# Layer 0's expert weights loaded in five transfers, four of them paced by the row scatters, and one program block for all parts behind attention 0

## The reference, cut to what matters

```python
for e in range(N_EXPERTS):                       # 16 experts, each token goes to 2
    h = silu(flat @ Wu[e]) * (flat @ Wg[e])
    out = out + combine[:, e:e + 1] * (h @ Wd[e])
for s in range(N_SHARED):
    out = out + silu(flat @ Su[s]) * (flat @ Sg[s]) @ Sd[s]
...
x = x + ffn0(layernorm(x))                       # layer 0, then
x = x + attn1(layernorm(x))                      # layer 1's attention
```

## Time and profile before

| what | value |
|---|---|
| time, median of 3 runs | 1125.06 us (1124.02 to 1129.27) |
| the profiled execution's own time | 1130.29 us |
| its span, from the first to the last instruction | 1128.6 us |
| PE busy | 889.0 us, 79% |
| DVE, POOL, ACT busy | 687.4, 632.6, 467.2 us |
| granted TensorE clock, mean | 0.849 |

### The profile page before, as it was taken

One profiled execution on the slowest core, in us unless ns is written; L12 is line 12 of the kernel. 1 busy time (PEld: TensorE's weight loads), 2 busy tenths in 40 slices (PEclk: granted clock), 3 DMA queues, 4 the chain that ended last, 5 costly groups with the idle time before them and its releaser, 6 DMA issues.

```text
span 1128.6 us, 22056 instructions
## 1 busy us (share of the span) xinstructions
PE 889.0 (79%) x5927; PEld 689.5 (61%) x5927; DVE 687.4 (61%) x2668; ACT 467.2 (41%) x1176; POOL 632.6 (56%) x878
## 2 busy tenths in 40 slices
PE   1578888888597899268888788997599999999900
PEld 0456666665554788156666556564488888888700
DVE  5688898774553355366788666354255555555578
ACT  2336566554310344145665444331144444444400
POOL 3646666533137356375558888877366665665600
PEclk9769899897889899556989877598699999999955
DMA  7600000000253553700001222277555555555287
GB/s 214 225 1 1 1 2 1 1 2 2 80 225 109 149 151 104 261 0 1 2 1 72 83 94 100 100 246 293 200 173 175 179 177 174 175 171 169 69 355 314
DMA packets 72965, 136.97 MB, mean 121 GB/s; under 512 B 13278, under 2 KB 51597, under 8 KB 70800
## 3 DMA queue, kind: packets, MB, share of 16 engines
q1 hardware_dynamic: 52016, 85.15, 23.3%
q0 software_dynamic: 17632, 46.73, 11.6%
q10 hardware_dynamic: 3200, 3.70, 0.9%
HBM read 79.15 MB, written 62.39 MB: 125 GB/s over the span
## 4 chain that ended last, share of the span: by engine, by line
PE 32%; POOL 11%; DVE 8%; issue 5%; DMA 2%; ACT 1%; POOLq 0%; DVEq 0%; SPq 0%; ACTq 0%
PE s_psum L2047 12%; POOL rows L1577 7%; PE s_psum L2060 6%; PE s_psum L2039 3%; DVE f_rows L2148 2%; DVE f_xT L2148 2%; DVE a_masked L1089 2%; PE s_psum L2055 2%; POOL a_probs L1436 1%; PE s_psum L649 1%; DMA rows<-f_rows,f_place_at 1%; PE s_psum L552 1%; PE s_psum L605 1%; PE s_psum L585 1%; PE s_psum L632 1%
## 5 line engine op out<-in xcount | busy, mean ns | idle before, releaser
L2159 POOL DMA_INDIRECT parts<-e_y,e_dest x206 | 202.6, 984 | 154.8 <-issue 121.6
L2047 PE MATMUL s_psum<-wres,e_xT 128*128 x824 | 215.1, 384 | 0.3 <-ACT e_xT L2088 0.2
L1436 POOL TENSOR_SCALAR_AFFINE_SELECT a_probs<-a_probs 128x256 f32<-128x256 f32 x256 | 108.7, 449 | 120.1 <-ACT a_probs L873 119.6
L2047 PEld LDWEIGHTS s_psum<-wres,e_xT 128*128 128x128 f32 x824 | 158.1, 193 | 22.6 <-issue 1.1
L1577 POOL DMA_INDIRECT rows<-f_rows,f_place_at x128 | 125.3, 979 | 36.3 <-issue 32.3
L873 ACT ACTIVATE a_probs<-s_psum 128x768 f32<-128x768 f32 x128 | 104.6, 817 | 75.2 <-PE s_psum L632 73.5
L2093 ACT ACTIVATE e_act_out<-s_psum 128x128 f32<-128x128 f32 x206 | 57.2, 278 | 178.1 <-PE s_psum L2047 178.1
L2122 DVE TENSOR_TENSOR e_hid<-e_act_out,s_psum 128x128 f32<-128x128 f32 x206 | 59.5, 289 | 113.2 <-PE s_psum L2055 84.2
L2060 PE MATMUL s_psum<-wres,e_hT 128*128 x412 | 123.6, 382 | 0.0
L1089 DVE CUSTOM_DVE_ANT_0 a_masked<-s_psum,a_ahead 128x128 f32<-128x128 f32 (+1 forms) x256 | 76.0, 353 | 42.7 <-PE s_psum L608 42.2
L2131 DVE TENSOR_SCALAR e_y<-s_psum,e_xg 128x256 f32<-128x256 f32 x206 | 99.7, 484 | 1.0 <-issue 1.0
(11 more groups left out here) (299 smaller groups left out, 1993.1 us busy)
## 6 DMA issues: line engine op xcount, KB each, us to landing
e_xg<-rows SPq DMA_DIRECT2D x159, 160.0 KB, 2.3
f_rows<-parts SPq DMA_DIRECT2D x8, 1024.0 KB, 7.3
f_xT<-parts SPq DMA_DIRECT2D x8, 1024.0 KB, 7.8
wres<-in_experts SPq DMA_DIRECT2D x21, 384.0 KB, 5.7
e_xg<-rows SPq DMA_DIRECT2D x47, 144.0 KB, 2.2
wres<-in_experts SPq DMA_DIRECT2D x4, 1536.0 KB
rows<-empty SPq DMA_DIRECT2D x1, 5120.0 KB, 24.5
parts<-e_y,e_dest POOLq DMA_INDIRECT x206, 2.4
```

The costliest lines, as they stand in the source:

```text
L1436: last = nc.gpsimd.affine_select(out=diagonal[:, :, a], in_=diagonal[:, :, a], compare_op=ALU.is_ge, fill=0.0, base=0, pattern=[[0, 2], [1 ...
L2047: last = nc.tensor.matmul(ps_u[b % 2][:, 0:2 * P], xT[b % 2][:, c * P:(c + 1) * P], wres[:, ds(e, 1), 2 * c * P:2 * (c + 1) * P].rearrange ...
L2159: nc.gpsimd.indirect_dma_start(out=parts[:, :], out_offset=bass.IndirectOffsetOnAxis(ap=dest[b % NY][:], axis=0), in_=y[b % NY][:], in_off ...
```

## The change

In `dispatch`, SP now loads experts 0 to 7 in one transfer at the stage's start, and experts 8 to 15 in four transfers of two experts (768 KB each). Before transfer n of these four it waits on `scattered[0]` for 16 * 3 * (n + 1), which is the landing of scatter 4, 10, 16 and 22. PE waits for five transfers in place of four (`wres_count` 80, was 64). Layer 0's dispatch and expert blocks and all of layer 1 stand in one program block, without the clearing and the barriers between. ACT's split of the bias gets a wait for the first results, which takes the barrier's place. POOL's four sums wait for all of the last four result loads, by one semaphore, in place of one each. Some semaphores are made only in the layer that uses them.

```diff
-    front = {"wres_loaded": wres_loaded, "wres_count": 64, "tab_done": tab_done, "scattered": scattered,
+    front = {"wres_loaded": wres_loaded, "wres_count": 16 * (1 + (E - EARLY_EXPERTS) // PIECE), "tab_done": tab_done, "scattered": scattered,
...
-        for q in range(4):
-            part = slice(q * E // 4, (q + 1) * E // 4)
+        sp.dma_start(wres[:, 0:EARLY_EXPERTS], w_all[0:EARLY_EXPERTS].rearrange("e p n -> p e n")).then_inc(wres_loaded, 16)
+        for n, first_expert in enumerate(range(EARLY_EXPERTS, E, PIECE)):
+            part = slice(first_expert, first_expert + PIECE)
+            sp.wait_ge(scattered[0], 16 * SCATTERS_PER_PIECE // 2 * (n + 1))
             sp.dma_start(wres[:, part], w_all[part].rearrange("e p n -> p e n")).then_inc(wres_loaded, 16)
...
             if front is not None:
+                act.wait_ge(env["results_loaded"][0], 16)
                 nc.scalar.activation(bias_hi[:], bias[0:1, :], ACT.Copy).then_inc(bias_hi_done, 1)
...
-                pool.wait_ge(env["results_loaded"][s], 16)
+                pool.wait_ge(env["results_loaded"][DVE_SUMS], 16 * (B - DVE_SUMS))
...
-        with nc.sbuf_tensor("wres0", [P, EXPERTS[0], WCOLS], F32) as wres:
-            env["wres"] = wres
-            with ExitStack() as keep, stage(nc, "s1_") as joined:
-                begun = dispatch(nc, env, 0, moe[0], dram[0], joined, keep, shared)
-                expert_blocks(nc, env, 0, dram[0], joined, begun)
-                env["results"] = begun["results"]
...
-            with stage(nc, "s2_") as joined:
-                make_sem, psum, _ = joined
+        with stage(nc, "s1_") as joined:
+            make_sem, psum, _ = joined
+            with nc.sbuf_tensor("wres0", [P, EXPERTS[0], WCOLS], F32) as wres:
+                env["wres"] = wres
+                with ExitStack() as keep:
+                    begun = dispatch(nc, env, 0, moe[0], dram[0], joined, keep, shared)
+                    expert_blocks(nc, env, 0, dram[0], joined, begun)
+                    env["results"] = begun["results"]
```

More of the change, by code:

```diff
@@ L47 @@
 IN_FLIGHT = 4
+EARLY_EXPERTS, PIECE, SCATTERS_PER_PIECE = 8, 2, 6
 DVE_SUMS = 4
@@ L422, in attention @@
         qk_ps = sem("qk_ps")
-        v_ps = sem("v_ps")
-        v_done = sem("v_done")
+        v_ps = sem("v_ps") if multi else None
+        v_done = sem("v_done") if multi else None
         var_ready = sem("var_ready")
         rstd_ready = sem("rstd_ready")
-        sq_done = sem("sq_done")
-        ss_done = sem("ss_done")
+        sq_done = sem("sq_done") if multi else None
+        ss_done = sem("ss_done") if multi else None
         raw_done = sem("raw_done")
-        scaled = sem("scaled")
+        scaled = sem("scaled") if multi else None
         rot_done = sem("rot_done")
@@ L460, in attention @@
         shared_loaded = sem("shared_loaded")
[L461 to L467, removed]
+        m_stats_done = sem("m_stats_done") if ahead_of_moe is not None else None
+        m_var_ready = sem("m_var_ready") if ahead_of_moe is not None else None
+        m_eps_done = sem("m_eps_done") if ahead_of_moe is not None else None
+        m_rstd_ready = sem("m_rstd_ready") if ahead_of_moe is not None else None
+        m_applied = sem("m_applied") if ahead_of_moe is not None else None
+        m_xT_ps = sem("m_xT_ps") if ahead_of_moe is not None else None
+        m_logits_ps = sem("m_logits_ps") if ahead_of_moe is not None else None
         bias_hi_done = sem("bias_hi_done")
@@ L474, in attention @@
         dve_ln = Chain(sem("dve_ln"), 1)
-        dve_rs = Chain(sem("dve_rs"), 2 + 3 * NEWTON)
+        dve_rs = Chain(sem("dve_rs") if multi else None, 2 + 3 * NEWTON)
         pool_ln = Chain(sem("pool_ln"), 2)
@@ L1868, in finish @@
         ps_l, ps_r = psum[:, 6], psum[:, 7]
-        ones_made = sem("ones_made")
         count_ps = sem("count_ps")
@@ L1934, in _ @@
             chain.start(0)
-            nc.vector.memset(ones[:], 1.0).then_inc(ones_made, 1)
-            dve.wait_ge(ones_made, 1)
+            step(nc.vector.memset(ones[:], 1.0))
             dve.wait_ge(count_ps, 1)
@@ L2002, in expert_blocks @@
         stored = [sem(f"stored{i}") for i in range(NY)]
[L2003 to L2006, removed]
+        if front is not None:
+            yk_loaded = [sem(f"yk_loaded{i}") for i in range(NC)]
+            summed = sem("summed")
+            sums = Chain(sem("sums"), 1000)
+            out_stored = sem("out_stored")
         def loaded(eng, b):
@@ L2026, in _ @@
                     sp.dma_start(begun["results"][m], parts[m * N * K:(m + 1) * N * K].rearrange("(t p k) n -> p t (k n)", p=P, k=K)
-                                 ).then_inc(env["results_loaded"][m], 16)
+                                 ).then_inc(env["results_loaded"][min(m, DVE_SUMS)], 16)
             for t in range(NT if front is not None else 0):
@@ L2141, in _ @@
                     weigh(i - 2, owner.pop(0))
-            sums.start(0)
+            if front is not None:
+                sums.start(0)
             for t in range(NT if front is not None else 0):
@@ L2195, in layers @@
         env["late_loaded"] = ctx.enter_context(nc.semaphore("late_loaded"))
-        env["results_loaded"] = [ctx.enter_context(nc.semaphore(f"results_loaded{m}")) for m in range(B)]
+        env["results_loaded"] = [ctx.enter_context(nc.semaphore(f"results_loaded{m}")) for m in range(DVE_SUMS + 1)]
         attn1, attn0, moe0 = ExitStack(), ExitStack(), ExitStack()
@@ new lines, in layers @@
+        with stage(nc, "s1_") as joined:
[6 more added lines that the diff above has]
+                    env["results"] = begun["results"]
+            moe0.close()
+            E = EXPERTS[1]
+            with ExitStack() as late:
+                front = {"rows": sb("f_rows", [P, NT, row_width(1)], F32, late), "xT": sb("f_xT", [P, FC, T], F32, late),
+                         "place_at": sb("f_place_at", [P, NT, 8], I32, late), "cum": sb("f_cum", [P, E], F32R, late),
+                         "router": moe[1]["router"], "router_bias": moe[1]["router_bias"], "const": moe[1]["const"],
+                         "table": dram[1]["rows"],
+                         "scattered": [late.enter_context(nc.semaphore(f"scattered{i}")) for i in range(IN_FLIGHT)],
+                         "ws": sb("f_ws", [P, 2, WCOLS], F32, late), "w_shared": dram[1]["shared"]}
+                env["wres"] = nc.alloc_sbuf_tensor_at("wres1", [P, E, WCOLS], F32,
+                                                      offset=nc.sbuf_usable_end // 32 * 32 - 4 * E * WCOLS)
+                front["w_experts"] = dram[1]["experts"]
```

## The result

The changed kernel took 1129.07 us in the median of 13 runs (1124.69 to 1137.74), the kernel before 1124.92 (1120.15 to 1130.09). The ratio is 1.0039, with a 95% interval from 1.002 to 1.0057: 4.4 us slower by the ratio (the two medians lie 4.2 apart), inside the bound of 0.5% that the prediction set for what can be told, but the measurement's own interval leaves no change out. The profiled execution of the changed kernel is the fastest of its runs, 1124.69 us with a span of 1123.0. It can't be set against the profiled one of before as a whole. In it attention 0 alone, which the change doesn't touch, ended 8.5 us earlier: SP issued the first load of the dispatch at 294.56 in place of 303.07. So all that follows compares spans inside the execution, from one event to another.

What follows compares the result with a forecast made beforehand. It took the dispatch to be bound by scatter landings, two in flight, and the border by the barrier. -2.9 (early load) + 6.0 (pieces) - 2.4 (barriers) = +0.7 us on 1125.06 gave 1125.8 us, range 1119.5 to 1130.6.

Steps and rivals of the forecast that it cites:

- No change to be told: Whole kernel: time stays within 0.5%, or 5.6 us, of the kernel before; chance 0.71.
- the early load: Dispatch start: queue empty 4 us before the first scatter, third scatter's wait falls from 3.34 to 0.48; -2.9 us.
- The price of a piece: Layer 0 dispatch: each of four 768 KB loads delays the scatters by 1.5 us, +6.0 us in all.
- the row of layer 1: A layer 1 scatter that met 384 KB loads landed in 4.3 us, not 2.5: 1.8 us late, a guide for the estimate.
- The 2.31 us without a cause: Dispatch before the change: POOL's wait at 335.76, with no large load under way and no cause found.
- the fourth rival: Dispatch: the unexplained wait at 335.76 goes and the loads are near free; sum -5.5 us, 1119.6 us; chance 0.09.
- The barriers: Layer border: DVE and ACT released by the first result load at 459.3, not 461.74; -2.4 us.
- POOL's common wait: After the border: POOL's sums wait for the last result load, with 7.5 us of cover; costs nothing.
- SP's late reading of the table: Dispatch: SP reads the block table only behind the fourth late weight load, with 12 us of cover; costs nothing.
- the clock: Attention 1: PE's rise from 1.2 GHz taken to move with the start; otherwise the border's gain changes by some us.
- Fair sharing: Dispatch: the late loads slip between scatters for 0.4 us each; sum -3.7 us, 1121.4 us; chance 0.27.
- The slower rival: Dispatch: each late load costs 3.1 us, what the first scatter lost; sum +7.1 us, 1132.2 us; chance 0.12.

Runs made afterwards that it cites:

- The runs with three and four in flight: Changed kernel, but scatter n of layer 0 waits for scatter n - 3 or n - 4, not n - 2; ratios to the kernel before 0.9968 and 0.99.
- the pieces alone: Kernel before plus the five weight transfers, four behind scatters, still two program blocks; timed twice, ratios 1.0026 and 1.0085.
- the one with all pieces in one row: Changed kernel, but all four 768 KB loads wait for scatter 4 only; ratio to the kernel before 1.004.
- the half-size run: Changed kernel, but twelve experts in the early transfer and four later loads of one expert (384 KB) each; ratio to the kernel before 0.9968.
- the block alone: Kernel before with the one program block, expert weights still in four transfers at the stage's start; timed twice, ratios 0.9992 and 0.9983.

## Why the prediction was right or wrong

**No change to be told: right, at the upper end.** 1129.07 us lies in the range of 1119.5 to 1130.6, and the ratio of 1.0039 inside 0.5%. The forecast was +0.7 us and the measurement +4.4. The bound of 0.5% itself was too wide: 13 runs of each tell 0.2%, and by them the change does make the kernel slower. That the number stayed in the range is in part luck. The pieces cost 4.0 us more than forecast and the early load gave 1.0 less; against this stood 1.8 us that the sum had not counted on (below) and 0.3 more from the border.

**The price of a piece was mis-sized: 2.5 us, not 1.5.** This is the step "I take 1.5, a little under the row of layer 1". The number and the mechanism were as written: piece and scatter issued together, two in flight, no slack. The place was two scatters off: 6, 12, 18 and 24 land late, but they start on time, and POOL stands idle before 8, 14, 20 and 26. The four waits add 10.0 us and not 6.0. Two reasons of the step failed. The engines were said to be "done 1.96 us after it starts, so a delay far above 2 is unlikely"; they were busy with the piece and the two scatters until 324, 4.8 us after its issue at 319.20, and the piece took an estimated 2.6 of all engines. And "part of the second scatter's delay can hide" was no reason: the first of the two is 2.5 late by itself (5.0 against 2.5), the second only 1.6 (4.1), and POOL feels the first in full. The runs with three and four in flight show that it is the wait for the landing that costs, and not POOL or the bytes.

**The early load gave 1.9, not 2.9, in the profiled execution.** The queue is empty 4 us before the first scatter, as worked out:

```profile
306.05:310.08 4.03, 4.03 (x7) 1.58 (x6) 2.98 (x21) 0.60 (x1) 0.00 (x0) 0.69 0.01 2
```

Yet the first scatter landed after 3.6 us, and the third waited 1.48 for it. In the first run of the pieces alone and in the one with all pieces in one row it waited 1.80 and 1.47. In the half-size run and in the second run of the pieces alone it waited the usual 0.5, which is the whole 2.9. What makes the first one late by 1.1 us in some executions stays open.

**The 2.31 us without a cause** is not in the changed kernel as a wait of its own. This makes up 1.8 us, which I had left out of the sum: -1.9 - 1.8 + 10.0 = +6.3, and the span shows +6.4. It does not look like an accident of one execution, as the fourth rival had it. The wait is there in all four runs with two in flight whose pieces don't fall on that place (2.31 before, 1.45 and 2.48 in the block alone, 2.15 with half-size pieces), and with full pieces it is gone or small (0.77 in the second run of the pieces alone); see the last section.

**The barriers: right.** -2.4 forecast, -2.7 seen: the first result landed after 3.5 us in place of 3.9. The run of the block alone has -2.5. POOL's common wait and SP's late reading of the table cost nothing, as said. Attention 1 took 345.1 us from DVE's first sum to the first block matmul, 345.7 before, and 84.7 us of expert blocks stand against 84.8. So the clock changed the sum by no more than 0.6 us, although it rose earlier behind the border. It went from 1.2 to 2.4 GHz (0.50 to 1.00) between 513 and 514 in the changed kernel, 57 us after DVE's first sum:

```profile
512.00:513.00 1.00, 1.00 (x7) 0.98 (x6) 0.85 (x5) 0.68 (x3) 0.77 (x2) 0.50 0.00 0
513.00:514.00 1.00, 1.00 (x14) 0.85 (x12) 0.34 (x3) 0.59 (x3) 0.49 (x3) 0.81 0.00 0
514.00:515.00 1.00, 1.00 (x19) 0.47 (x17) 1.00 (x9) 1.00 (x4) 0.83 (x2) 1.00 0.00 0
```

Before, it did so between 522 and 523, 61 us after the sum:

```profile
522.00:523.00 1.00, 1.00 (x11) 0.81 (x11) 0.36 (x3) 0.19 (x1) 1.00 (x3) 0.72 0.03 8
523.00:524.00 1.00, 1.00 (x11) 1.00 (x9) 0.84 (x6) 0.82 (x1) 0.82 (x2) 1.00 0.06 16
```

**The rivals.** Fair sharing falls: 2.5 us a piece and not 0.4, though the whole price is not a full queue's 3.1 either. By the rule of the Trainium skill (DMA: Bandwidth & Descriptors, queues, rings and completion order) a scatter has its turns between the piece's packets. The traces don't show the order of the packets. The run with all pieces in one row agrees with the rule, as its scatter 6 landed with more than 4 us of load to come. But the turns don't keep a scatter from landing only when a single piece is through: 324.45 against 319.20 + 4.8 = 324.0. The slower rival would have needed 2.7 us a piece, with the early load's 2.9; the price came within 0.2 of it.

## What to carry to other kernels

A load that is released by the same semaphore as the small transfer that you mean to spare will meet it every time, as it did here four times of four. No run released the pieces at another point between two scatters, so whether that is cheaper is not shown. Before you place a load among latency-bound transfers, work out the slack: the number in flight by the issue pace (here 2 x 1.26, 3 x 1.26, 4 x 1.26 us) against the landing time under load (4.5 to 5.4 us). Raising the first from 2 to 4 took the dispatch from 58.4 to 45.2 us with the pieces and from 51.5 to 44.4 without them, and then it hardly mattered where the load stood. With the block and the pieces together it made the kernel 1.0% faster than the one before. A barrier between stages can go where the first transfer of the next stage orders the work anyway; it gives back the time between that landing and the barrier's end, 2.5 us here.

## What the runs showed of the hardware

**A load's first microsecond moves little.** From 320 to 321 us the engines were 81% busy at 98 GB/s, and at the start of a load of 384 KB in layer 1, from 782.0 to 782.5 in the trace before, they were full at 80 GB/s. So a count of bytes at 401 GB/s gave too short a time for the piece of 768 KB, 1.96 us against the estimated 2.6. The price to the scatters did not go by the count of transfers: a piece of 384 KB made a scatter's successor wait 1.0 us more than usual, one of 768 KB 2.5.

**A fetch of instructions may hold up a scatter.** In each of the eleven traces there is one transfer on an instruction queue (q8) 13 to 17 us after the first scatter. The DMA queues of the kernel before from 331.6 to 333.6 us (packets, MB, share of 16 engines):

```profile
q0 software_dynamic: 68, 0.17, 25.5%
q8 instruction: 1, 0.02, 4.9%
```

4.9% of 16 engines over 2 us are 1.57 us of one engine, in one packet. The scatter then under way, started at 331.04, landed after 4.5 us, which is the wait of 2.31 at 335.76. A wait of the same kind stands 16.5 to 17.0 us after the first scatter in the block alone (1.45 and 2.48) and with half-size pieces (2.15); with four in flight no wait over 0.73 is seen. With full pieces it mostly falls together with one of theirs. That the fetch is the cause fits in place and size, but no run moved or removed it, so it is not shown.
